# Normalised rows left by each block for the next, in an eight-block float32 model kernel

## What is computed

```python
x = x + attn_a(ln(x), Wqkv, ...)      # causal, 16 heads, ALiBi bias
x = x + ffn_L0(ln(x), ...)            # silu gate MLP + product-key experts, top 8
x = x + softmax(ln(x)^T ln(x))-mix    # attention over the 256 features
x = x + ffn_L0(ln(x), ...)            # the same weights again
x = x + attn_L1(ln(x), ...)           # rotary, 4 key heads
x = x + ffn_L1(ln(x), ...)            # gate MLP with 2:4 sparsity
x = x + scan_L1(ln(x), ...)           # running maximum and complex prefix product
x = x + ffn_L1(ln(x), ...)
```

## Time and profile before

| | us |
|---|---|
| median of 3 runs | 1620.43 (1616.7 to 1627.98) |
| the profiled execution's own time | 1619.1 |
| its span, first to last instruction | 1617.3 |
| TensorE busy | 1384.7 (86%) |
| VectorE busy | 1073.8 (66%) |
| ScalarE busy | 623.9 (39%) |
| GpSimd busy | 346.3 (21%) |

### The profile page before, as it was taken

How to read it: one execution, slowest core, us unless ns; L and a number is a source line. 1 busy time by engine, 2 the same in 40 slices (tenths; PEclk the granted TensorE clock), 3 DMA queues, 4 the chain that set the end, 5 groups by cost and what they waited for, 6 DMA issues and landing times. The chain is left out here.

```text
span 1617.3 us, 20802 instructions
## 1 busy us (share of the span) xinstructions
PE 1384.7 (86%) x7632; PEld 970.3 (60%) x7632; DVE 1073.8 (66%) x2187; ACT 623.9 (39%) x1159; POOL 346.3 (21%) x301
## 2 busy tenths in 40 slices
PE   3889999588999678899966899999779889889897
PEld 2545554267888567788852334333258667677676
DVE  5656555387678448767738566667266568898775
ACT  1354444353333224333321555556642334333321
POOL 3311100162433102243331340400040201020010
PEclk9799999789999898999986999999989989999899
DMA  6715320220000000000004413210000000000000
GB/s 144 97 29 73 52 30 2 81 71 1 1 1 1 1 1 1 1 1 1 0 34 49 89 32 58 30 21 2 1 1 1 1 0 1 1 0 1 14 13 26
DMA packets 32173, 39.03 MB, mean 24 GB/s; under 512 B 5986, under 2 KB 27210, under 8 KB 31946
## 3 DMA queue, kind: packets, MB, share of 16 engines
q1 hardware_dynamic: 32074, 37.73, 13.1%
HBM read 14.45 MB, written 2.10 MB: 10 GB/s over the span
## 5 line engine op out<-in xcount | busy, mean ns | idle before, releaser
L1302 DVE TENSOR_REDUCE attn_negm<-ps 128x2 f32<-128x1024 f32 (+3 forms) x256 | 255.9, 1021 | 88.6 <-PE ps L916 46.2
L1127 ACT ACTIVATE attn_probs<-ps 128x512 f32<-128x512 f32 (+3 forms) x512 | 237.1, 515 | 177.6 <-PE ps L944 100.0
L480 POOL TENSOR_TENSOR moe_h_low<-moe_h,moe_h_high 128x512 fp32r<-128x512 f32 x96 | 137.0, 1430 | 316.5 <-ACT moe_h_high L430 316.5
L936 PE MATMUL ps<-attn_qs,attn_ks 99*128 99x512 bf16 (+4 forms) x512 | 153.6, 347 | 30.7 <-ACT attn_probs L1127 18.9
L916 PE MATMUL ps<-attn_ks,attn_qs 96*128 96x512 bf16 (+4 forms) x512 | 142.4, 362 | 31.0 <-DMA attn_ks<-attn_part 20.9
L447 ACT ACTIVATE moe_silu<-ps 128x512 f32<-128x512 f32 x96 | 57.5, 599 | 235.1 <-PE ps L353 234.9
L1685 PE MATMUL ps<-sb_f_down,tail_h 128*128 128x256 f32 x512 | 123.2, 386 | 7.1 <-DVEq L1978 7.1
L936 PEld LDWEIGHTS ps<-attn_qs,attn_ks 102*128 102x128 bf16 (+1 forms) x512 | 49.1, 97 | 126.9 <-ACT attn_probs L1127 100.5
L957 PE MATMUL ps<-attn_probs,attn_va 128*32 128x512 f32 (+3 forms) x1024 | 118.3, 535 | 0.0
L1685 PEld LDWEIGHTS ps<-sb_f_down,tail_h 128*128 128x128 f32 x512 | 98.2, 193 | 24.2 <-DVEq L1978 7.3
L1951 DVE TENSOR_TENSOR tail_h<-tail_silu,ps 128x512 f32<-128x512 f32 x64 | 43.6, 682 | 89.5 <-PE ps L1675 57.3
(11 more groups left out here) (324 smaller groups left out, 3302.4 us busy)
## 6 DMA issues: line engine op xcount, KB each, us to landing
attn_qs<-attn_part SPq DMA_DIRECT2D x96, 128.0 KB, 4.4
attn_ks<-attn_part SPq DMA_DIRECT2D x48, 128.0 KB, 6.2
out_x<-x SPq DMA_DIRECT2D x4, 512.0 KB, 2.7
x<-in_x SPq DMA_DIRECT2D x1, 1536.0 KB, 9.7
attn_ks<-attn_part SPq DMA_DIRECT2D x24, 64.0 KB, 4.6
moe_raw<-in_f_gate SPq DMA_DIRECT2D x2, 512.0 KB, 6.8
moe_raw<-in_f_up SPq DMA_DIRECT2D x2, 512.0 KB, 8.0
moe_raw<-in_f_down SPq DMA_DIRECT2D x2, 512.0 KB, 8.6
```

What stands on the lines that cost most here:

```text
L480: pool.tensor_tensor(hc.low[:, j % RING, :], h[:, j % RING, :], hc.high[:, j % RING, :], ALU.subtract).then_inc(low_done, 1)
L936: last = pe.matmul(ps[:, SC + k, 0:width2(kt)], ks[0:ROWS2, b % 2, hd % KH, kt * P:(kt + 1) * P], qs[0:ROWS2, b % 2, hd, T - width2(kt):T] ...
L1127: act.activation(pr[:, s2 % RING, j, 0:n], ps[:, SC + k, 0:n], ACT.Exp, scale=HD ** -0.5).then_inc(exp_done, 1)
L1302: dve.tensor_reduce(m, ps[:, 2 * half:2 * half + 2, 0:width1(qt)], AX, ALU.max, negate=True).then_inc(r1_free, 1)
```

## The change

One `xn` of two slots now lies in SBUF for the whole run, and each stage but the last leaves normalised rows in it for the stage that follows: those of `following`, which is [0, 2] ahead of an expert stage and [0] ahead of any other. The following stage computes no first rows, and VectorE only increments the semaphore that says they are there.

- Expert stages leave after products 5, 6 and 7 of batch 3 (statistics in the first part, one batch's rows in each of the others). Their own opening keeps the statistics of batches 1 and 3.
- Attention stages leave in the three steps behind step 64, once the last addition to the highest batch in `following` is done. In attn1 the opening increments `xn_ready` behind the three memsets; attn0, whose input has just been loaded, is as it was at its start.
- The feature stage keeps its rolled loop and leaves both batches ahead of its last addition.
- In moe0 the last two weight pieces are loaded into the two slots of the shared `xn` (as before they lay over `xn`), and `CUTS_BEFORE_ROWS` is 0: the two row copies stand ahead of all cuts, six cuts ahead of the query copies.
- In the last stage ScalarE makes two cuts, the row copies, then two cuts; the low halves of the weights move from GpSimd to VectorE, two ahead of the rows' low halves and two behind.

```diff
@@ expert_feed_forward
-        nb = [NormBuffers(Scope(nc, f"{name}_norm{i}", stack), 2 * NT) for i in range(2)]
+        nb, nb_next = (NormBuffers(Scope(nc, f"{name}_norm{i}", stack), tiles * NT) for i, tiles in enumerate((2, len(following))))
+        xn = g["xn"]
-        if parts:
-            place_raw(range(N_WTS, len(parts)))
-        xn = s.sb("xn", [P, 2, NT, D])
+        for k in range(N_WTS, len(parts)):
+            raw[k] = xn[:, k - N_WTS, :, :].rearrange("p t d -> p (t d)").rearrange("p (c f) -> p c f", c=parts[k][1].high.shape[1])
-        CUTS_BEFORE_ROWS, CUTS_BEFORE_CHUNKS = 3, 6
+        CUTS_BEFORE_ROWS, CUTS_BEFORE_CHUNKS = 0, 6
...
+            def leave(part):
+
+                if part == 0:
+                    dve.wait_ge(x_done, max(following) + 1)
+                    dve.wait_ge(transposed, B)
+                    ce = Chain(dve, next_steps, NormBuffers.steps(len(following) * NT))
+                    ce.start(0)
+                    tile_stats(dve, ce, x, [NT * f + t for f in following for t in range(NT)], nb_next)
+                elif part <= len(following):
+                    norm_apply(dve, x, following[part - 1], nb_next, xn[:, part - 1, :, :], NT * (part - 1))
+
+            dve.sem_inc(xn_ready, 2)
+            for k in range(2):
+                take(k)
             cn = Chain(dve, norm_steps, NormBuffers.steps(2 * NT))
-            for i in range(2):
-                cn.start(i)
-                tile_stats(dve, cn, x, [NT * ROWS[2 * i + k] + t for k in range(2) for t in range(NT)], nb[i])
-                if i == 0:
-                    for k in range(2):
-                        norm_apply(dve, x, ROWS[k], nb[0], xn[:, k, :, :], NT * k).then_inc(xn_ready, 1)
-                    for k in range(2):
-                        take(k)
-                else:
-                    dve.tensor_scalar(minus[:, :], nb[1].mv[:, :, 0], -1.0, None, ALU.mult).then_inc(stats_ready, 1)
+            cn.start(0)
+            tile_stats(dve, cn, x, [NT * ROWS[k] + t for k in (2, 3) for t in range(NT)], nb)
+            dve.tensor_scalar(minus[:, :], nb.mv[:, :, 0], -1.0, None, ALU.mult).then_inc(stats_ready, 1)
...
+                    if b == B - 1 and 5 <= j < 8:
+                        leave(j - 5)
@@ attention
-        xn = s.sb("xn", [P, NT, D])
+        xn = g["xn"][:, 0]
...
+            def leave(part):
+
+                if part == 0:
+                    dve.wait_ge(free["dve"], jobs.count[("out", max(following), 1)])
+                    dve.wait_ge(ready, jobs.number[("rows", B - 1, DC - 1)])
...
             if causal:
                 dve.wait_ge(x0_in, 16)
-            c0 = Chain(dve, norm0_steps, NormBuffers.steps(NT))
-            c0.start(0)
-            norm_stats(dve, c0, g, 0, nb0)
-            c0.end()
-            norm_apply(dve, x, 0, nb0, xn).then_inc(xn_ready, 1)
+                c0 = Chain(dve, norm0_steps, NormBuffers.steps(NT))
...
+            else:
+                dve.sem_inc(xn_ready, 1)
...
+                if STEPS < t <= STEPS + 3:
+                    leave(t - STEPS - 1)
@@ feature_attention
-            normalise(0)
-            norm_apply(dve, x, 0, nb, xn).then_inc(xn_ready, 1)
+            dve.sem_inc(cn.sem, NormBuffers.STEPS)
+            dve.sem_inc(xn_ready, 1)
...
             batch_row(B - 1, None, B - 2)
+            dve.wait_ge(x_done, B)
+            dve.wait_ge(tr_ready, B)
+            ce = Chain(dve, next_steps, NormBuffers.steps(len(following) * NT))
+            ce.start(0)
+            tile_stats(dve, ce, x, [NT * f + t for f in following for t in range(NT)], nb_next)
+            for k, f in enumerate(following):
+                norm_apply(dve, x, f, nb_next, g["xn"][:, k], NT * k)
             add_to_x(B - 1)
@@ feed_forward_and_scan
-        xn = {"f": s.sb("xnf", [P, NT, D]), "s": s.sb("xns", [P, NT, D])}
+        xn = {"f": g["xn"][:, 0], "s": g["xn"][:, 1]}
...
-            for n, at in parts:
+            for n, at in parts[:2]:
                 act.activation(halves[n].high[at], raw[n][at], ACT.Copy).then_inc(w_high, 1)
             act.wait_ge(consts, 1)
             for job in early:
                 do(job)
+            for n, at in parts[2:]:
+                act.activation(halves[n].high[at], raw[n][at], ACT.Copy).then_inc(w_high, 1)
...
-            pool.wait_ge(xn_ready["f"], 1)
-            for k, (n, at) in enumerate(parts):
-                pool.wait_ge(w_high, k + 1)
-                pool.tensor_tensor(halves[n].low[at], raw[n][at], halves[n].high[at], ALU.subtract).then_inc(w_low, 1)
...
+            def low_part(k):
+                n, at = parts[k]
+                dve.wait_ge(w_high, k + 1)
+                dve.tensor_tensor(halves[n].low[at], raw[n][at], halves[n].high[at], ALU.subtract).then_inc(w_low, 1)
...
-            c0 = Chain(dve, n0_steps, NormBuffers.steps(NT))
-            c0.start(0)
-            tile_stats(dve, c0, x, range(NT), nb0)
-            norm_apply(dve, x, 0, nb0, xn["f"]).then_inc(xn_ready["f"], 1)
+            dve.sem_inc(xn_ready["f"], 1)
+            for k in range(2):
+                low_part(k)
             for job in early:
                 do(job)
+            for k in range(2, len(parts)):
+                low_part(k)
@@ stages
+        xn = stack.enter_context(nc.sbuf_tensor("xn", [P, 2, NT, D], F32))
```

40 lines of the change are left out of this document (26 added, 14 removed).

## The result

Measured: 1598.33 us median (1593.86 to 1600.34, 4 runs) against 1624.2 for the kernel before beside it, ratio 0.9839 with a 95% interval of 0.9804 to 0.9875. Measured again later, beside other kernels: 1599.95 (1596.41 to 1603.39, 6 runs), ratio 0.9859 [0.9834, 0.9884]. The forecast was 1590.8, a gain of 29.6 us; the medians say 26 and 22. Both medians lie in the range of 1582 to 1603, and even the fastest run, 1593.86, is above the forecast itself. The profiled execution is that run, with a span of 1592.1 us at a mean granted clock of 0.946 (1617.3 and 0.938 before).

What follows compares the result with a forecast made beforehand. TensorE's time plus its stalls is the span, with long waits for VectorE's normalised rows at stage openings. Gains 6.3 + 7.4 + 3.7 + 6.3 + 5.9 = 29.6 us off 1619.1, plus 1.3 to the median, give 1590.8; range 1582 to 1603.

Steps and rivals of the forecast that it cites:

- Attention to experts, 6.3: First expert stage's opening: rows lie ready, TensorE transposes at once, first down matmul about 344.4 for 350.71; won 6.3 us.
- Rival 1: First expert stage: weight landings, query copies behind six cuts and stretched statistics eat the 6.3 us; 1597 us, chance 0.18.
- The stretched statistics: First expert stage's opening: VectorE's statistics slow to about one small step per GpSimd operation, done by 331, before 333.
- Experts to feature stage, 7.4: Feature stage's opening: first energy matmul 5.7 us sooner, its sixteen matmuls another 1.7 quicker; won 7.4 us.
- Feature stage to experts, 3.7: Into the second expert stage: of 8.6 us moved, 3.7 comes back as delay of the last addition; won 3.7 us.
- Experts to attention, 6.3: Second attention's opening: rows are released behind the three memsets at 829.4, first transpose before at 835.73; won 6.3 us.
- Attention to last stage, 5.9: Last stage's opening: first chunk at 1179.3 instead of 1185.25, with two weight low parts on VectorE ahead; won 5.9 us.
- Leaving costs nothing in the tuned loops: Attention and expert stages: VectorE's idle time covers leaving; product 6 of batch 3 2 to 3 us late, costed at nothing.
- rival 2: Four tuned loops: leaving isn't covered, 25.7 us come back, 1616.5 us; chance 0.08 (fully or mostly).
- Rival 4: Whole kernel slower: denser TensorE work lowers its granted clock everywhere, 1649 us at a mean of 0.90; chance 0.02.

Runs made afterwards that it cites:

- second trace of before: The kernel before, profiled once more with no edit, to learn the scatter of stage lengths: 1627.3 us in its one run.
- no_leave: Changed kernel with all leaving but the first attention's taken out, so next stages take stale rows: 1592.46 us median, ratio 0.9799.
- tail_pool: Changed kernel with the last stage's weight low halves back on GpSimd and all four ScalarE cuts ahead of the row copies: 1597.14 us, ratio 0.9837.

## Why the prediction was right, and where it was not

1. *Attention to experts, 6.3.* The stage is 4.2 to 6.6 us shorter, so the size holds. The points on the way: first gate matmul 17.4 after the stage's start (forecast 18.5), first product 21.7 (22.8), first down matmul 34.1 (34.2). Two steps were wrong, so that the size holds is in part luck. TensorE ran at the high level from its first transpose, and the 1.7 us (transposes) and 2 us (queries) that this saved went into a longer wait, 6.40 for 3.2, at the query copy. And the down matmul is not the point that sets the stage's end; VectorE's chain up to the queries of batch 1 is, and it came 5.2 to 6.7 sooner. Rival 1, that weights and query copy hold this opening, was right in part: with the copy early the stage gives 3.4 more. The stretched statistics were foreseen, their end at 20.8 us behind the stage's start, measured 19.7. By the Trainium skill (SBUF — State Buffer, Who interferes with whom) the later of the two engines waits for the whole of the earlier's instruction. The trace agrees: 2.27 for a step of 0.17, beside 2.35. But the price did not go when the statistics went, as other operations took it over.
2. *Experts to feature stage, 7.4.* Right: the first maxima 7.4 sooner (11.8 to 4.3), 8.6 against the second trace of before.
3. *Feature stage to experts, 3.7.* Right in the two parts taken together: from the feature stage's start to the next stage's first product it was 79.6 and 82.7 us, and is 70.1, 9.5 and 12.6 less for a forecast of 11.1. What was missed is TensorE's idle 5.22 behind VectorE's straight line (8.97 before), which the sum gave no price; no_leave shows that the low level behind it still costs 2.5 us.
4. *Experts to attention, 6.3.* Right at the opening (13.2 to 6.8 is 6.4). Over the whole stage it was 4.4 in the first pair of traces and 7.3 in the second. At 88 us into the stage the changed kernel's traces lead the first trace of before by 4.4 to 4.8 us, and the second by 6.8 to 7.2; behind that point only the steps of 1.6 us come and go, in traces of either kernel.
5. *Attention to last stage, 5.9.* 6.3 and 6.0 at the first product, 6.5 and 6.7 at the end. Right in size, wrong in one reason: the sum had the weights' low halves on VectorE in the path, and tail_pool shows that where they are made matters to no more than 0.6 us.
6. *Leaving costs nothing in the tuned loops.* Right (no_leave); rival 2 is out. Product 6 of batch 3 is some 3 us late, as forecast, and TensorE is not idle behind it. Rival 4 is out too: the mean granted clock rose, to 0.946 and 0.943. One reading of the waits was wrong and changes nothing: in the last stage the wait for rows (7.0 us) was not the longest; one of 8.0 us comes later, and stays (7.9).

The sum over the stages behind the first is 27.4 in the first pair of traces and 30.7 in the second, against 29.6. The time came out 7.5 to 9 us above the forecast for two other reasons. The forecast's base was the median of three runs, 1620.4, while beside the changed kernel the kernel before had medians of 1624.2 and 1622.4; and the gain by medians is 22 to 26. For the first measurement that is 3.8 us by the base and 3.7 by the gain. In the first pair of traces, 2.2 us are lacking in the stages behind the first, and the first attention, which the sum did not touch, ran 2.1 longer. The rest of the 4 to 7 us between 29.6 and the gain by medians is of the size by which single traces of one kernel differ here, and it was not split further.

## What to carry to other kernels

Work moved from the head of a stage into another engine's shadow at the end of the one before is won at its full length, as long as that shadow is there; where it is not (the feature stage), count the idle time that it puts in front of TensorE as well as its own length. To price an opening, find the matmul behind which the stage has the same length in every run, and follow its chain: points ahead of it can move by 6 us and count for nothing. A constant distance alone doesn't prove it, as the first down matmul had one too until an edit moved it away from VectorE's chain. And one profiled execution of the second attention is worth no more than plus or minus 3 us. Compare such stages by several traces, or matmul by matmul, where steps of equal size at the same places are the clock's and not the edit's.

## What the runs showed of the hardware

- Beside back-to-back GpSimd subtractions of 128x1024 (2.3 to 2.5 us each), some short VectorE operations move at one for each GpSimd operation: inverse-root steps (2.27 for 0.17) and a copy (2.50 for 0.28). Others are not held up: eight maxima of 0.21 to 0.23 us ran beside one such subtraction. The same weights' low halves take 2.36 on GpSimd and 1.23 on VectorE, both inputs in SBUF.
- The granted clock of the same opening is not the same in every run. With 1.94 us of idle in front (1.97 in one), the first energy product was at the high level in ten traces and partly at the low one in one; with 2.63 the transposes of the second expert stage were low each time and the queries high once and low twice.
- In the second attention the clock falls to the low level for short stretches, though TensorE is busy throughout (6.00 of 6.00 us in the rows above), as it is in the traces where the clock stays high; in the 9 us ahead it is busy for 8.7 in both traces. Each costs 1.6 us, and which traces of one kernel have them differs.
- The first attention, the same code in all traces up to its leaving, ended between 308.9 and 316.4 us. In the trace that ended first, TensorE was granted the low level for 20.5 us of it, in the one that ended last for 40.9.
